# Unrolling two attention stages into 32 units, with one sum of four heads' outputs and column-tiled score and sum products

## The reference

```python
x = x + L0_xattn(_layernorm(x), ctx, ctx, mask, wq, wk, wv, wo)     # 32 heads over 8 kv heads, head size 128
x = x + L0_ffn(_layernorm(x), w_gate, w_up, w_down)                 # 512 -> 1376 -> 512
x = x + L1_xattn(_layernorm(x), ctx, Wq, Wk, Wv, Wo, q_norm_w, k_norm_w)
x = x + L1_ffn(x, gamma, beta, w1, b1, w3, b3)
```

```python
q = (query @ wq) ; k = (key @ wk) ; v = (value @ wv)        # 4 query heads share one kv head
raw  = einsum('bhqd,bhkd->bhqk', rope(q), rope(k)) / sqrt(128) + mask
out  = einsum('bhqk,bhkd->bhqd', softmax(raw), v).reshape(bs, sq, 4096) @ wo
```

## Time and profile before

| | us |
|---|---|
| median of 3 runs (1688.03 to 1689.34) | 1688.38 |
| the profiled execution's own time | 1689.24 |
| its span, first to last instruction | 1687.5 |
| first attention, eight kv heads | 32.7 to 615 |
| second attention, eight kv heads | 832 to 1605 |
| PE busy | 1552.7 (92%) |
| DVE, ACT, POOL busy | 1029.0, 606.8, 562.1 |

### The profile page before, as it was taken

One profiled execution on the slowest core, in us unless ns is written; L12 is line 12 of the kernel. 1 busy time (PEld: TensorE's weight loads), 2 busy tenths in 40 slices (PEclk: granted clock), 3 DMA queues, 4 the chain that ended last, 5 costly groups with the idle time before them and its releaser, 6 DMA issues. The chain is left out here.

```text
span 1687.5 us, 27752 instructions
## 1 busy us (share of the span) xinstructions
PE 1552.7 (92%) x9485; PEld 1351.2 (80%) x9488; DVE 1029.0 (61%) x2126; ACT 606.8 (36%) x1430; POOL 562.1 (33%) x458
## 2 busy tenths in 40 slices
PE   4999999999999979989599999999999999999925
PEld 3888878888888868868498989888898989888823
DVE  5758576685857785666645364554545354544687
ACT  2222222222222234431335353534435343444446
POOL 3434434343353415542322212223221322222146
PEclk9999999999999989999699999999999999999959
DMA  6011111111111002210300101110010101110021
GB/s 179 28 36 31 47 34 37 37 31 31 31 50 41 3 20 75 74 33 1 112 26 15 42 12 31 31 31 25 25 37 6 38 24 31 31 31 0 0 75 50
DMA packets 81134, 63.03 MB, mean 37 GB/s; under 512 B 7280, under 2 KB 66928, under 8 KB 81104
## 3 DMA queue, kind: packets, MB, share of 16 engines
q1 hardware_dynamic: 80240, 62.47, 12.7%
q10 hardware_dynamic: 864, 0.20, 0.1%
HBM read 60.56 MB, written 2.10 MB: 37 GB/s over the span
## 5 line engine op out<-in xcount | busy, mean ns | idle before, releaser
L127 POOL TENSOR_TENSOR att_w_lo<-att_w_raw,att_w_hi 128x512 fp32r<-128x512 f32 x160 | 206.4, 1306 | 202.4 <-ACT att_w_hi L122 202.4
L70 PE MATMUL att_proj<-att_w_hi,kv_hi 128*128 128x256 f32 x768 | 220.3, 287 | 11.3 <-DVEq L41 11.3
L763 DVE TENSOR_TENSOR x_rows<-att_proj,x_rows 128x512 f32<-128x512 f32 x256 | 172.8, 686 | 85.5 <-PE att_proj L70 82.1
L70 PE MATMUL att_proj<-att_w_hi,kv_lo 128*128 128x256 f32 x768 | 219.3, 285 | 0.0
L70 PE MATMUL att_proj<-att_w_lo,kv_hi 128*128 128x256 f32 x768 | 219.2, 285 | 0.0
L70 PE MATMUL att_proj<-att_w_hi,att_o_hi 128*128 128x512 f32 x512 | 211.4, 413 | 0.2
L988 POOL TENSOR_TENSOR att_probs<-att_probs,att_total 128x512 f32<-128x512 f32 x64 | 82.8, 1294 | 378.0 <-DVE att_total L744 378.0
L70 PE MATMUL att_proj<-kv_hi,att_w_hi 128*128 128x512 f32 x512 | 206.6, 404 | 0.0
L70 PE MATMUL att_proj<-att_w_lo,att_o_hi 128*128 128x512 f32 x512 | 201.7, 394 | 0.0
L70 PE MATMUL att_proj<-att_w_hi,att_o_lo 128*128 128x512 f32 x512 | 201.2, 393 | 0.0
L70 PE MATMUL att_proj<-kv_lo,att_w_hi 128*128 128x512 f32 x512 | 200.2, 391 | 0.0
(11 more groups left out here) (150 smaller groups left out, 2946.9 us busy)
## 6 DMA issues: line engine op xcount, KB each, us to landing
att_w_raw<-in_wq SPq DMA_DIRECT2D x64, 256.0 KB, 2.7
att_w_raw<-in_wo SPq DMA_DIRECT2D x64, 256.0 KB, 2.8
ln_stage<-in_ctx_t SPq DMA_DIRECT2D x8, 512.0 KB, 5.3
att_w_raw<-in_wk SPq DMA_DIRECT2D x16, 256.0 KB, 2.8
att_w_raw<-in_wv SPq DMA_DIRECT2D x16, 256.0 KB, 3.1
ffn_w_raw<-in_gate_t SPq DMA_DIRECT2D x10, 256.0 KB, 2.9
ffn_w_raw<-in_up_t SPq DMA_DIRECT2D x10, 256.0 KB, 3.1
ffn_w_raw<-in_down_t SPq DMA_DIRECT2D x10, 256.0 KB, 3.0
```

What stands on the lines that cost most here:

```text
L70: last = eng.matmul(out, a, b, start=(first and n == 0), stop=(n == 3 * len(terms) - 1))
L127: eng.tensor_tensor(self.lo[:, slot], self.raw[:, slot], raw(self.hi[:, slot]), ALU.subtract)\
L763: eng.tensor_tensor(st.x[:, row], proj[job % 4][:], st.x[:, row], ALU.add)\
```

## The change

Both attentions are written out without loops. Work is numbered in 32 units, u = 4g + n for kv head g; n // 2 is now the half of the sequences and n % 2 the pair of query heads. All semaphore targets become constants. Within a unit the order is new: `scores(u)`, a filling of projections, `turn(u)`, one `q_job` of unit u+2, `weigh(u)`, the other `q_job`. The filling is for n = 0 the four output jobs of the head before, second half; for n = 1 the kv jobs of this head's second half (2 in the first attention, 4 in the second); for n = 2 the output jobs of the first half; for n = 3 the kv jobs of the next head's first half. In units 0 and 1 it is half of the second half's kv jobs each.

- An output job now sums four query heads (12 matmuls), so there are 8 of them for each kv head rather than 16, and as many `add_out`.
- The weights' high and low parts have a place of their own for each of 10 chunks, the raw ones 4 slots; the chunks are rounded and split one unit or more before use.
- Keys are turned half by half in the `att` banks (`turn_keys`), in the first attention right after `turn(u)`, in the second after `weigh(u)`, for u odd. The keys before the scores are in `k_rows`, a buffer of their own.
- In the first attention a score matmul of 128 output rows becomes two of 64 (columns 0 to 63 and 64 to 127 of the array). In the second, each of the 8 sum matmuls becomes four of 32 output rows.
- The last step of `rsqrt` is chained by its caller.

The core of the diff ("..." marks what is left out):

```diff
...
+            def q_sums(u):
...
+                for b in range(NBH):
+                    for r in range(4):
+                        rows, g, part = slice(32 * r, 32 * r + 32), r // 2, slice(32 * (r % 2), 32 * (r % 2) + 32)
+                        last = eng.matmul(proj[job % 4][rows, b:b + 1], squares[:, u % 2, b, g, part], st.ones[:, 0:1],
+                                          start=True, stop=True)
+                last.then_inc(proj_full, 1)
...
+            def turn_keys(g, h):
+                for i in range(TKH):
...
+                        eng.wait_ge(k_scaled, TKH * (2 * g + h) + i + 1)
+                    turned, out = att_room("key", g, h, i)
+                    need(eng, turned_copied, turned)
+                    need(eng, out_drained, out)
...
+            def scores(u):
...
+                        if rope:
+                            for a in range(2):
+                                last = eng.matmul(sco[job % 2][S * a:S * a + S, cols], q_cols[:, u % 4, b, a, :],
+                                                  k_cols[:, key], start=True, stop=True)
...
+            def project(g, h, t):
+                job = proj_job["out", g, h, t]
+                eng.wait_ge(w_split, weights.ready(g, C_O + GROUP - 1))
+                eng.wait_ge(out_drained, 2 * (4 * g + 2 * h + 2))
...
+                    for a in range(GROUP)]).then_inc(proj_full, 1)
...
+            for u in range(UNITS - 2):
+                work = filling(*divmod(u, 4))
+                scores(u)
+                fill(work[0])
+                q_sums(u + 1)
+                for what in work[1:]:
+                    fill(what)
+                if early_q(u):
+                    q_job(u + 2, 0)
+                turn(u)
+                if rope and keys_after(u):
+                    turn_keys(*keys_after(u))
+                q_job(u + 2, 1 if early_q(u) else 0)
+                weigh(u)
+                if not rope and keys_after(u):
+                    turn_keys(*keys_after(u))
+                if not early_q(u):
+                    q_job(u + 2, 1)
+            u, g = UNITS - 2, NKV - 1
+            scores(u)
...
+            project(g, 0, 2)
+            scores(u + 1)
+            turn(u)
+            project(g, 0, 3)
+            weigh(u)
+            turn(u + 1)
+            weigh(u + 1)
+            for t in range(4):
+                project(g, 1, t)
```

`early_q(u)` holds in the first attention for odd u, and for u < 2 in both. DVE's order (`take` is `add_out` or the taking of keys, whose last one of a half in the second attention contains the 11-step chain):

```diff
+            for u in range(UNITS - 2):
+                work = filling(*divmod(u, 4))
+                scale_scores(u)
+                take(work[0])
+                q_means(u + 1)
+                for what in work[1:-1]:
+                    take(what)
+                add_up(u)
+                if len(work) > 1:
+                    take(work[-1])
+                q_refine(u + 1)
+                take_q(u + 2, 0)
+                if early_q(u):
+                    take_q(u + 2, 1)
+                out_low(u)
+                if not early_q(u):
+                    take_q(u + 2, 1)
```

POOL's order:

```diff
+                for what in work[:-1]:
+                    rotate(*what)
+                normalise(u)
+                for what in work[-1:]:
+                    rotate(*what)
+                if keys_after(u):
+                    scale_keys(*keys_after(u))
...
```

More of the change, by code:

```diff
@@ L320, in attention @@
     KL = S if rope else 2 * S
[L321 to L339, removed]
+    KVH = NBH * KL // (2 * P)
+    TKH = NBH * KL // BANK
+    SJ = TJ = TKH
+    UNITS = 4 * NKV
+    w_hi, w_lo, w_split = weights.hi, weights.lo, weights.split
+    def filling(g, n):
+        def keys(g, h):
+            return [("kv", g, h, j) for j in range(KVH)]
+        def outs(g, h):
+            return [("out", g, h, t) for t in range(4)]
+        if g == 0 and n < 2:
+            return keys(0, 1)[KVH // 2 * n:KVH // 2 * (n + 1)]
+        if n == 0:
+            return outs(g - 1, 1)
+        if n == 1:
+            return keys(g, 1)
+        if n == 2:
+            return outs(g, 0)
+        return keys(g + 1, 0) if g + 1 < NKV else []
@@ new lines, in attention @@
+    number("q", 1, 1)
+    for i in range(TKH):
+        number_att("key", 0, 0, i)
+    for u in range(UNITS):
+        g, n = divmod(u, 4)
+        for i, what in enumerate(filling(g, n)):
+            number(*what)
+            if i == 0 and not rope and u + 1 < UNITS:
+                number("sum", u + 1)
+        if u + 2 < UNITS:
+            number("q", u + 2, 0), number("q", u + 2, 1)
+        new_keys = (g, 1) if n == 1 else (g + 1, 0) if n == 3 and g + 1 < NKV else None
+        for i in range(TJ):
+            number_att("turn", u, i)
+        if rope and new_keys:
+            number_att("key", *new_keys, 0)
+        for i in range(2):
+            number_att("out", u, i)
+        if not rope and new_keys:
+            for i in range(TKH):
+                number_att("key", *new_keys, i)
@@ L341, in attention, with keys_after, early_q @@
+    for t in range(4):
+        number("out", NKV - 1, 1, t)
+    att_kind = list(att_job)
+    def keys_after(u):
+        g, n = divmod(u, 4)
+        return (g, 1) if n == 1 else (g + 1, 0) if n == 3 and g + 1 < NKV else None
+    def early_q(u):
+        return rope and u % 2 == 1 or u < 2
     with ExitStack() as ctx:
@@ L835, in _ @@
-            with eng.Fori(0, NKV - 1) as it:
-                head(it, False)
-            head(NKV - 1, True)
+            for j in range(KVH):
+                take(("kv", 0, 0, j))
+            take_q(0, 0); take_q(0, 1)
+            take_q(1, 0)
+            q_means(0)
+            take_q(1, 1)
+            q_refine(0)
+            for u in range(UNITS - 2):
[15 more added lines that the diff above has]
+                    take_q(u + 2, 1)
@@ L839, in _ @@
+            u, g = UNITS - 2, NKV - 1
+            scale_scores(u)
+            add_out(g, 0, 0)
+            q_means(u + 1)
+            add_out(g, 0, 1)
+            add_up(u)
+            q_refine(u + 1)
+            add_out(g, 0, 2)
+            scale_scores(u + 1)
+            add_out(g, 0, 3)
+            out_low(u)
+            add_up(u + 1)
+            out_low(u + 1)
+            for t in range(4):
+                add_out(g, 1, t)
         @block.scalar
         def _(eng):
-            if not rope:
-                sco_drained.start(eng)
```

1041 lines of the change are left out of this document (446 added, 595 removed).

## The result

The changed kernel takes 1730.8 us (median of 4 runs, 1729.7 to 1732.2), the kernel before 1688.2 on the same chip: a ratio of 1.025, 95% interval 1.0235 to 1.027. It is slower by 43 us; 1724 had been forecast. The profiled execution has a span of 1728.8 us.

A forecast was written before the change was run, and what follows sets the result against it. PE's instruction stream, busy 92% of the span, was taken as the bound. From 1689.2 us, +3.4 for the first attention and +31.3 for the second gave 1723.9, stated as 1724; range 1672 to 1772.

The forecast's parts named there:

- Sums: Second attention: a column-tiled block of sums takes 0.65 us rather than 1.70, gaining 33.6 us in 32 units.
- Rival 2: Column tiles don't overlap: sums take 2.0 us rather than 0.65, scores 2.0 rather than 1.1; 1781 us; chance 0.2.
- Scores: First attention: column-tiled scores take 1.1 us rather than 1.7, 2.4 a head, half handed back after odd units.
- New wait 2: Second attention, odd units: turn_keys waits for DVE's out_low, behind q_refine; 4.2 us with the turn, 15 times, 62 us.
- New wait 1: First attention: PE idles 1.6 us before output jobs after odd units, 0.25 after even ones; 3.7 a head.
- Edges: The first and last units have too little filling work: 9 us in the first attention, 7 in the second.
- Clock: Second attention: idle stretches bring falls of the granted clock to 1.2 GHz, 15 at 0.9 us: 13.5 us.
- Rival 3: The stream starves: fetching and issuing 128 instructions makes a sum take 4.4 us; +119, 1840 in all; chance 0.05.
- Rival 1: Second attention's keys don't wait long: no POOL-DVE collision, clock holds: 1684 us, or 1648 with DVE also early; chance 0.22.

The follow-up runs named there:

- after_keys_late_pool: The changed kernel with one wait added: in the second attention POOL's scale_keys waits until DVE has ended q_refine(u+1); 1692.9 us, ratio 1.0028 to the kernel before.

## Why the prediction was right, step by step

The direction, the mechanism and the size hold: 1730.8 against 1724, or 42.6 us more than before against 34.7. The sum had +3.4 for the first attention and +31.3 for the second. To compare, the first attention takes 585.4 us (31.2 to 616.6) against 582.3, so +3.1; the second 811.9 (833.0 to 1644.9) against 772.3, so +39.6.

- **Sums**: 0.65 forecast, 0.64 measured; 33.6 us forecast for 32 blocks, 32.6 measured by undoing them, of which some 30 are the blocks. Rival 2, that column tiles load one after another, is out. The trace differs from the rule of the Trainium skill that stood beside it (TensorE: Matmul & The Clock Gate, "The mechanism" in Part 3): by it the sums would have taken 2.0 us, by the prediction's estimate. **Scores**: 1.1 and 1.08. That half is swallowed behind odd units holds: 9 us measured in the pairs (5.6 in the whole kernel) for what I put at 19.2 less half.
- **New wait 2**: by exactly the steps named: the keys' chain, `q_refine` with two steps held by POOL (1.8 forecast, 1.65 measured, 1.59 by taking it away), `take_q`, `out_low`. The 3.9 forecast is the time by which PE leaves later, not PE's idle time. To compare: PE goes from `weigh` to the job behind `turn_keys` in 6.21 us (1094.75 to 1100.96), where 1.70 for `weigh` and 0.8 for the transposes would be 2.5, so 3.7 are lost, of which 3.28 are idle and the rest is a slower end and start. With 0.3 at the turn it is 4.0 for the 4.2 forecast (15 times 4.2 is 63; the sum has 62). The undisturbed head is 97.66 us; the sum without clock and edges gives 96.3 + (62 + 1.6 + 1.6 - 33.6 - 20.8)/8 = 97.65. The terms are off by tenths on both sides (even units' turn, put at 0.1, doesn't wait at all), so that these agree to 0.01 is luck.
- **New wait 1**: 1.6 forecast, 16 times; 1.38 measured, 15 times, and 2.02 at the end; even units 0.25 forecast, 0.02 measured. The head is 71.2 (twice 35.58) rather than 71.6, 3.5 us less in eight.
- **Edges, mis-sized in the first attention**: its eight heads at 71.16 leave 16 us of its 585.4; the kernel before has 582.3 - 578.4 = 3.9 by its 72.3, of which 1.6 are two clock falls. So the new order's edges cost 14, not 9. The last units alone have 3.96 us ahead of turn(31), 0.73 ahead of weigh and 2.02 ahead of the output jobs, much of it at half clock. That the sum of this stage came out right to 0.3 us is luck: 5 us more of edges against 3.5 less in the heads and 1.6 for the old kernel's two falls, which the sum left out.
- **Clock, the term that was too small**: 13.5 forecast as 15 falls at 0.9 us. That 0.9 was a single row from a stretch of long matmuls. Here falls cost 1.6 at 3.4 us and 2.5 to 2.7 at 6.8, and five of twelve are long: 21 us. That leaves 8 of the second attention's +39.6 for the edges (39.6 - 8 x 1.36 - 21), forecast at 7: 5.22 us ahead of turn(31) and 1.46 ahead of the last output jobs are among them. The bound of 1.7 for a fall that PE works through was the better value; no row of the kernel before showed a fall of 6.8 us inside the attentions.
- **Rival 3**, the stream starving: 128 instructions of a sum went through in 0.64 us, and no wait for fetching shows inside the attentions.
- **Rival 1** was the right alternative to name. It did not happen here; one move of `q_refine` brings its two conditions about, no collision ahead of `out_low` and a steady clock. That this kernel's 1679 lies near its 1684 is chance: 1684 still had waits of 2.4 us in it, and here they are 0.96.

What the prediction didn't ask is what the tiles do without the new order. It took their gain as PE's own because PE was busy 92% of the time. In the old order more than half of the gain goes to waits that grow as the blocks ahead of them shrink (1.9 of 4.2 us a head in the second attention, nearly all of 2.5 in the first), and with tiled sums some 10 us more to new falls of the clock.

## What to carry to other kernels

When PE is over 90% busy, shortening one of its blocks still pays only up to the next semaphore: count for each block how far ahead of PE its releaser is, and follow that releaser's own in-order list, where ten steps of 0.2 us can be worth 50. Try the order of the small operations on the helping engines first, since it is the cheapest edit (four moved lines: 19 us here, 34 with the tiles), and try each part of a combined change alone and in both orders. Idle stretches of 3 us on PE should be priced with the clock that follows them: here 48 us of waits at `turn_keys` brought some 21 us of slow clock.

## What the runs showed of the hardware

- Column tiles of 32 columns load and run side by side: 64 weight loads and 64 one-column matmuls in 0.64 us, 10 ns for each pair (16 of 128 columns: 1.70). Two tiles of 64 columns and 64 streamed columns: 32 pairs in 1.08 us.
- Small DVE operations that read SBUF alone stand still while POOL works, up to 1.03 us for one of 0.17; with an input in PSUM they don't (two of `out_low` took 1.28 beside POOL in `after_keys_late_pool`, 1.29 in the earlier trace rows). Delaying POOL by 1.9 us made the kernel 38 us faster.
- Falls of the granted clock to 1.2 GHz in the second attention, by the wait that they followed: behind ten of the fourteen waits of 3.3 to 3.5 us in the changed kernel, behind four of fourteen of 1.6 to 1.9 with POOL held back, and behind none of the like waits of 0.74 to 0.78 with `q_refine` early, in the same order of matmuls. In the old order: behind six of eight waits of 2.2 to 2.5 with tiled sums, four of eight with both tilings, and none of 1.38 (the kernel before) or 1.43 (`out_low` early).
- The length of the wait alone doesn't decide it: in the first attention the kernel before had two falls, each behind a wait of 0.86 (440.9 and 150.8 us), while in the changed kernel fifteen waits of 1.38 brought none from 78 to 596 us.
- A fall of 3.4 us cost 1.6 us in the second attention and 0.8 in the first of the kernel before (heads of 73.13 and 72.33); one of 6.8 cost 2.5 to 2.7.
